# All probabilities of an attention stage turned by VectorE and memory instead of half of them by TensorE

## The reference, cut to what matters

```
x   [16, 256, 256]    ctx [16, 256, 192]    16 heads of 64
q = layernorm(x) @ w_q ; k = ctx @ w_k ; v = ctx @ w_v
attn = softmax(q k^T / 8)                     # per sample and head [256, 256]
x = x + (attn @ v) @ w_o + b_o
x = x + ffn(layernorm(x))                     # 8 experts, the top 2 of each token, 640 slots an expert
```

## Time and profile before

| what | value |
|---|---|
| median of three runs | 955.93 us |
| the profiled execution | 957.82 us, its span 956.1 us, granted clock 0.992 |
| TensorE busy | 918.1 us (96%) |
| VectorE busy | 739.8 us (77%) |
| ScalarE busy | 573.8 us (60%) |
| GpSimd busy | 280.2 us (29%) |
| DMA queue of the SP (and any other hardware queue) | 122.87 MB, 42.9% of 16 engines' span |

### The profile page before, as it was taken

One profiled execution on the slowest core, in us unless ns is written; L12 is line 12 of the kernel. 1 busy time (PEld: TensorE's weight loads), 2 busy tenths in 40 slices (PEclk: granted clock), 3 DMA queues, 4 the chain that ended last, 5 costly groups with the idle time before them and its releaser, 6 DMA issues.

```text
span 956.1 us, 22462 instructions
## 1 busy us (share of the span) xinstructions
PE 918.1 (96%) x7916; PEld 821.0 (86%) x7916; DVE 739.8 (77%) x1745; ACT 573.8 (60%) x1600; POOL 280.2 (29%) x441
## 2 busy tenths in 40 slices
PE   7999999999999999999999999999889999999995
PEld 7878888888888888888888888888689999999995
DVE  5757778888888888888888888877777877678762
ACT  5877766667667666766766677676534433334420
POOL 5541112314233231323223132302533223322233
PEclk9999999999999999999999999999899999999999
DMA  8462535445455445455444445444345765645422
GB/s 239 143 205 91 163 123 163 162 152 168 146 157 158 148 157 164 136 172 164 139 156 161 146 130 170 136 134 136 121 133 99 149 145 123 135 84 98 112 29 27
DMA packets 152991, 133.29 MB, mean 139 GB/s; under 512 B 62140, under 2 KB 141610, under 8 KB 152752
## 3 DMA queue, kind: packets, MB, share of 16 engines
q1 hardware_dynamic: 144048, 122.87, 42.9%
q0 software_dynamic: 8832, 8.98, 5.4%
HBM read 82.15 MB, written 54.61 MB: 143 GB/s over the span
## 4 chain that ended last, share of the span: by engine, by line
PE 70%; DVE 11%; ACT 10%; issue 4%; DMA 3%; POOL 0%; SPq 0%; POOLq 0%; ACTq 0%; DVEq 0%
PE psum L734 20%; PE psum L839 9%; PE psum L996 9%; PE psum L855 9%; PE psum L980 8%; PE psum L801 7%; ACT prob L1067 6%; PE psum L819 5%; DVE negmax L1255 3%; DVE hidl L1201 2%; DVE bufl L1201 1%; ACT probt L1007 1%; DVE hidh L1488 1%; PE psum L879 1%; DVE psum L1274 1%
## 5 line engine op out<-in xcount | busy, mean ns | idle before, releaser
L1067 ACT ACTIVATE prob<-psum,negmax 128x256 f32<-128x256 f32 x512 | 238.0, 481 | 79.5 <-DVE negmax L1255 79.4
L1255 DVE TENSOR_REDUCE negmax<-psum 128x2 f32<-128x512 f32 x256 | 160.4, 682 | 29.7 <-PE psum L801 29.7
L1173 ACT ACTIVATE hid<-psum,b1t 128x640 f32<-128x640 f32 x64 | 50.9, 795 | 126.6 <-PE psum L980 125.0
L839 PE MATMUL psum<-probt,v 128*64 128x256 f32 x1024 | 124.6, 385 | 0.0
L707 POOL DMA_INDIRECT out_rows<-y,rowi x40 | 66.3, 1658 | 160.8 <-DVE y L1498 154.2
L1067 ACT ACTIVATION_READ_ACCUMULATOR prob<-psum,negmax 128x1 f32 x512 | 109.5, 214 | 0.0
L839 PEld LDWEIGHTS psum<-probt,v 128*64 128x64 f32 x1024 | 67.8, 136 | 36.4 <-issue 0.3
L668 POOL DMA_INDIRECT slot_table<-row,picki x64 | 66.8, 1044 | 96.9 <-PE psum L734 61.2
L996 PE MATMUL psum<-w2h,hidh 128*128 128x256 f32 x320 | 91.4, 286 | 2.9 <-DVE y L1498 1.5
L801 PE MATMUL psum<-kh,qh 64*128 64x256 f32 x512 | 82.5, 316 | 11.1 <-ACT prob L1067 8.9
L996 PE MATMUL psum<-w2l,hidh 128*128 128x256 f32 x320 | 90.5, 283 | 0.0
(11 more groups left out here) (199 smaller groups left out, 2704.6 us busy)
## 6 DMA issues: line engine op xcount, KB each, us to landing
squares<-prob SPq DMA_DIRECT2D x56, 512.0 KB
probt<-squares SPq DMA_DIRECT2D x224, 128.0 KB, 2.8
invrows<-inverses SPq DMA_DIRECT2D x128, 128.0 KB
w1r<-in_w SPq DMA_DIRECT2D x8, 1024.0 KB
w2r<-in_w SPq DMA_DIRECT2D x8, 1024.0 KB, 9.1
slot_table<-blank SPq DMA_DIRECT2D x8, 662.5 KB, 6.5
blocks<-slot_table SPq DMA_DIRECT2D x56, 80.0 KB
xin<-in_x SPq DMA_DIRECT2D x16, 256.0 KB, 3.5
```

The lines of the kernel that those rows point to most:

```text
L839: mm = pe.matmul(dst[h * HD:(h + 1) * HD, cc * S:(cc + 1) * S], v[:, b % 2, kb, cols], p, start=(kb == 0), stop=(kb == ST - 1))
L1067: last = act.activation(into, out_of, ACT.Exp, bias=negmax[:, m % 2, u, qb:qb + 1], accum_out=total[:, m % 2, u, qb:qb + 1])
L1255: dve.tensor_reduce(negmax[:, m % 2, u, :], psum[:, u, :].rearrange("p (q s) -> p q s", q=ST), AX.X, ALU.max, negate=True).then_inc(sem("m ...
```

## The change

Every unit of a period in `MOVED` is now turned by VectorE and memory; `by_pe` returns no unit there. What goes with it:

- `turn2`, `turn3`, `copy2`, `copy3` are gone from these periods. `square(m, pair)` transposes two units at once (1024 columns instead of 512), `lift` writes all four (1 MB instead of 512 KB), and each DMA of the move has 256 KB instead of 128 KB.
- The move of period m is issued in period m+1, two of its DMAs by SP (`move_low`, after `inv_out`) and two by ScalarE (`move_high`, between `q_hi` and `exp2`). The lift is now SP's last step of a period, behind `inv_in`; the residual traffic stands between the move and `inv_in`.
- `exps` waits for the lift of m-2, not for its move.
- `a_norm` writes to a new SBUF tensor `attended` (one buffer) instead of back to PSUM, stands behind `k_lo`, and waits for the `a_lo` of the period before. `a_hi` is copied from `attended`, behind `exp3`. `a_lo` of periods 4 to 59 is done by GpSimd.
- `ln1` from the third batch on and all of `pick` but its two reductions (`extremes`) go to GpSimd as well.
- Bank 4, where the turns were, becomes a fourth work bank; `places()` gives the banks out in turn and `pv`'s bank is free after `a_norm` instead of `a_lo`. `logits` uses a work bank too. `pv(m-2)` stands behind `k(m+1)` on TensorE.
- `c0`, `c1` have one buffer instead of two; the scatter waits for `k` instead of `q`.

The diff, cut to its core:

```diff
 def by_pe(m):
-    return (2, 3) if m in MOVED else (0, 1, 2, 3)
+    return () if m in MOVED else (0, 1, 2, 3)
...
         else:
-            out += [("q", m + 1), ("turn2", m - 1), ("k", m + 1), ("turn3", m - 1), ("v", m)]
+            out += [("scores", m)] + ([("logits", b - 2)] if r == 3 and 2 <= b else [])
+            out += [("q", m + 1), ("k", m + 1), ("pv", m - 2), ("v", m)]
...
         else:
-            out += [("copy2", m - 1), ("k_hi", m + 1), ("exp2", m), ("copy3", m - 1), ("exp3", m), ("v_sb", m)]
+            out += [*steps("exp0 exp1", m), ("q_hi", m + 1), ("move_high", m - 1), ("exp2", m), ("k_hi", m + 1), ("exp3", m),
+                    ("a_hi", m - 2), ("v_sb", m)]
...
+        else:
+            out += [("inv", m - 1)] + ([("slot", b - 3)] if r == 2 and 3 <= b else [])
+            out += [("bias", b - 2)] if r == 3 and 2 <= b else []
+            out += [("q_lo", m + 1), ("square0", m), ("k_lo", m + 1), ("a_norm", m - 2)]
         out += [("square1", m)] if m in MOVED else []
...
+        out += [("ln1", b + 1)] if r == 0 and 1 <= b < B - 1 else []
         out += [("scatter", b - 4)] if r == 0 and 4 <= b else []
         out += [("residual", b + 1)] if r == 0 and 1 <= b < B - 1 else []
+        out += [("a_lo", m - 2)] if m - 2 in POOL_REST else []
...
-        out += steps("inv_out inv_in", m - 1) + (steps("lift move", m) if m in MOVED else [])
+        out += [("inv_out", m - 1)] + ([("move_low", m - 1)] if m - 1 in MOVED else [])
+        out += [("traffic", b - 2)] if r == 1 and 2 <= b else []
+        out += [("inv_in", m - 1)] + ([("lift", m)] if m in MOVED else [])
...
+        def move(eng, m, groups):
+            eng.wait_ge(sem("lifted"), 16 * (m - MOVED[0] + 1))
+            eng.wait_ge(sem("pv"), m - 1)
+            for g in groups:
+                eng.dma_start(probt_all(m)[g * SQ:(g + 1) * SQ, :].rearrange("j (a c) -> j a c", a=GROUPS),
+                              square_table[m % 2].rearrange("(a j) (g c) -> g j a c", a=GROUPS, g=GROUPS)[g])\
+                   .then_inc(sem(f"moved{m % 2}"), 16)
...
-                sp.dma_start(square_table[m % 2], prob_pair(m)).then_inc(sem("lifted"), 16)
+                sp.dma_start(square_table[m % 2], prob_all(m)).then_inc(sem("lifted"), 16)
...
+            def a_lo(m):
+                pool.wait_ge(sem("a_hi"), m + 1)
...
+                pool.tensor_tensor(al[:, b % 2, c:c + 2, :], attended[:, :, :],
+                                   ah[:, b % 2, c:c + 2, :].bitcast(F32), ALU.subtract).then_inc(sem("a_lo"), 1)
...
-                if m >= 2 and u in by_pe(m - 2):
+                if m >= 2 and m - 2 not in MOVED:
                     act.wait_ge(sem("turn"), turns_to(m - 2, u))
                 elif m >= 2:
-                    act.wait_ge(sem(f"moved{m % 2}"), 16 * moves_to(m - 2))
+                    act.wait_ge(sem("lifted"), 16 * (m - 2 - MOVED[0] + 1))
...
                 dve.wait_ge(sem("inv_in"), 32 * (m + 1))
-                dve.tensor_tensor(at, at, invrows[:, :, :], ALU.mult).then_inc(sem("a_norm"), 1)
+                if m >= 1:
+                    dve.wait_ge(sem("a_lo"), m)
+                dve.tensor_tensor(attended[:, :, :], work_bank("pv", m).rearrange("p (c s) -> p c s", c=2),
+                                  invrows[:, :, :], ALU.mult).then_inc(sem("a_norm"), 1)
...
-                at = prob_pair(m).rearrange("p (g u c) -> p u g c", g=GROUPS, u=2)[:, u]
+                dve.wait_ge(sem("exp"), UNITS * m + 2 * pair + 2)
+                at = prob_all(m).rearrange("p (g v c) -> p v g c", g=GROUPS, v=2)[:, pair]
                 dve.transpose(at, at).then_inc(sem("square"), 1)
```

More of the change, by code:

```diff
@@ L118, in timeline @@
         out += [("pos", b - 3)] if r == 1 and 3 <= b else []
-        out += steps("exp0 exp1", m) + ([("a_hi", m - 2)] if m >= 2 else []) + [("q_hi", m + 1)]
         if four:
+            out += steps("exp0 exp1", m) + ([("a_hi", m - 2)] if m >= 2 else []) + [("q_hi", m + 1)]
             out += [("copy0", m - 1), ("exp2", m), ("k_hi", m + 1), ("copy1", m - 1), ("exp3", m), ("copy2", m - 1),
@@ L182, in timeline @@
             ("logits_part", o1), ("spread", 0), ("spread", 1), ("pos", e), ("base", 0), ("spread", 2), ("spread", 3)]
[L183 to L184 removed]
+    out += [*steps("exp0 exp1", m), ("q_hi", z), ("move_high", m - 1), ("exp2", m), ("k_hi", z), ("exp3", m), ("a_hi", m - 2), ("v_sb", m), ("x2t_sb", c), ("w_hi", 0), ("w_hi", 1),
             *steps("exp0 exp1", z), ("a_hi", m - 1), ("copy0", m), ("exp2", z), ("copy1", m),
@@ L228, with places @@
 WORKS = [w for w in WORKS if w not in APART]
-WORK_READ = {"xt": "xt_lo", "q": "q_lo", "k": "k_lo", "v": "v_sb", "pv": "a_lo", "o": "x2", "x2t": "x2t_sb",
+WORK_READ = {"xt": "xt_lo", "q": "q_lo", "k": "k_lo", "v": "v_sb", "pv": "a_norm", "o": "x2", "x2t": "x2t_sb",
              "logits": "biased", "pos": "slots"}
+def places():
+    banks, last, found = [5, 6, 7], {}, {}
+    for stage, n in TIMELINE:
+        work = stage.removesuffix("_most"), n
+        if (stage, n) == ("turn0", PERIODS - 2):
+            banks.remove(4)
+            found[stage, n] = 4, last[4]
+        if work in WORKS and work not in found:
+            at = banks.pop(0)
+            banks.append(at)
+            found[work] = at, last.get(at)
+            last[at] = work
+        if (stage, n) == ("turn3", MOVED[0] - 1):
+            banks.append(4)
+    return found
+PLACES = places()
 def build(nc, x, ctxt, wq, wk, wv, wo, bo, rw, rb, w1, b1, w2, b2, out):
@@ L685, in _ @@
                     inverse_root(stage[:3], n)
+                if stage == "ln1" and n >= 2:
+                    ln1(n)
+                if stage == "a_lo" and n in POOL_REST:
+                    a_lo(n)
+                if stage == "pick" and n < B - 4:
+                    pick_(n)
                 if stage == "vsplit":
@@ L1453, in _ @@
             for stage, n in TIMELINE:
-                if stage in steps:
+                if stage in steps and not (stage == "ln1" and n >= 2 or stage == "a_lo" and n in POOL_REST
+                                               or stage == "pick" and n < B - 4):
                     steps[stage](n)
```

174 lines of the change are left out of this document (97 added, 77 removed).

## The result

The changed kernel takes **1038.78 us** (median of four runs, 1029.57 to 1042.66); the kernel before took 955.52 beside it. The ratio is **1.0859** (95% interval 1.0784 to 1.0934): 8.6% slower, where 951 with a range to 986 was forecast.

What follows compares the result with a forecast made beforehand. The prediction took TensorE to bound the kernel before, then a loop through the lift: periods of 10.3, 10.8, 10.5 and 10.1 make 41.7 us a batch against 42.03, saving 4.6 us over 14 batches: 951 us, range 920 to 986.

Steps and rivals of the forecast that it cites:

- the circle: Loop from one move's issue through ScalarE, VectorE, SP and the lift to the next move: 10.1 us a period.
- TensorE's pace: Rival: TensorE still bounds after losing its turns, 38.5 us a batch, 907 us in all; chance 0.05.
- VectorE's sum: VectorE's work per batch: larger squares offset by work given to GpSimd, staying near 35.5 us of 42.
- the way from move to lift: Move's release to lift's issue, through ScalarE's issues, exp2, k_hi, then k_lo, a_norm, inv_in: 5.1 us with semaphores.
- the way from lift to move: Issue of the 1 MB lift to issue of the next move: 5.0 us, from 3.65 for 512 KB.
- The price by bytes: Lift's second 512 KB priced at the 386 GB/s seen in the middle of a lift: 1.36 us more.
- I take 0.7, nearer 0, as the engines are half idle: Delay of one lift a batch by 768 KB of residual traffic ahead of inv_in, bounded by 0 and 2.0 us.
- The share of 0.51: Share of the 16 DMA engines already in use before the change, about half the time over a batch.
- VectorE's own loop: Second loop in VectorE's order: 7.8 us plus small steps; 10.3 us where m mod 4 = 0, 10.5 where 2.
- the lift lands later: Rival: doubled bytes on shared DMA engines make lifts exceed 5.2 us; at 5.7, 982 us; chance 0.30.
- The GpSimd rival: VectorE's a_norm waits for GpSimd's late a_lo, stuck behind scatters and residual; 1 us late gives 965 us; chance 0.07.
- By bytes that becomes about 0.8: Within the late-lift rival: the DMA engines' busy share rises from 0.51 to about 0.8 with twice the bytes.

Runs made afterwards that it cites:

- e10: Kernel of e9 with ScalarE's half of the move left out, so half of the turned probabilities are never read back: 899.99 us, ratio 0.9428.
- e2: Changed kernel with the residual traffic issued behind the lift instead of ahead of inv_in, in periods with m mod 4 = 1: 1018.89 us, ratio 1.0674.
- e3: Changed kernel with VectorE applying ln2 ahead of k_lo instead of behind square1, in periods with m mod 4 = 2: 1007.66 us, ratio 1.0559.
- e11: Changed kernel with 12 identity transposes on TensorE that compute nothing, ahead of x2t's wait for ln2: 1019.20 us, ratio 1.0668.
- e4: Changed kernel with a_lo on VectorE again, behind square1; ln1 and pick stay on GpSimd: 1044.29 us, ratio 1.0925.
- e9: Kernel of e7, plus GpSimd's a_lo ahead of the scatters (periods with m mod 4 = 0) and a_hi ahead of move_high: 980.12 us, ratio 1.0274.
- e12: Changed kernel with only GpSimd's a_lo put ahead of the scatters, in periods with m mod 4 = 0: 1047.47 us, ratio 1.0958.
- e7: Changed kernel with the edits of e2 and e3, and move_high behind exp3 instead of ahead of exp2: 975.08 us, ratio 1.0210.
- e1: Changed kernel with all four pieces of the move issued by SP, none by ScalarE: 1016.04 us, ratio 1.0651.

## Why the prediction was wrong

**Right: TensorE does not set the pace any more, and the circle does, in three of its four steps.** The chain, the waits and the landings show it. The price of TensorE's pace was right as well: 38.06 us a batch in e10, where 38.5 was worked out, and 900 us against 907.

**Right: VectorE's sum** is 35.96 us a batch (35.57 before), the square 1.24, a_lo 1.28.

**Nearly right: the way from move to lift**, 5.5 us in the mean where 5.1 was summed; 1.7 us a batch.

**Wrong, the step that failed: the way from lift to move, "Then the lift itself", with 5.0.** It is 6.5 in the mean. Three parts:
- r3 and r0 took 5.2 and 5.8. The price by bytes was short by 0.2 to 0.8; why r0's lift lands 0.5 us later than r3's stays open. The Trainium skill's fit ("DMA: Bandwidth & Descriptors", Anatomy of one DMA) with 4.4 was further off than the rows' 5.0; the page gives it for DMAs that GpSimd issues, and SP issues these.
- r1: "I take 0.7, nearer 0, as the engines are half idle". It was 1.8 (e2), near the bound of 2.0. The share of 0.51 was a batch's mean, and from the kernel before. In the stretch in question, the 4.8 us ahead of r1's lift, the engines are full (1.02 from 398.5 to 403.3). A mean share says when nothing is missing over a batch; it does not say that there is room at a given place.
- r2: 8.0, of which 3 us were no lift at all (it landed after 4.8; e3). The prediction closed VectorE's own loop with ln2 in r2 as a small step behind square1 and priced its length, 10.5 us for the step where 13.3 was measured. It did not ask who waits for ln2: TensorE's x2t, and behind it the scores of r3. With the circle late, that small step came late, and the clock fell on top (20 us by e11).

These terms close the sum: the measured 48.2 us a batch is 6.5 over the forecast's 41.7, 91 us in 14 batches, and 951 + 91 = 1042.

**The rival "the lift lands later"**, chance 0.30, with 982 us at 5.7 us a lift, had the direction and a part of the size. Lifts landed after 5.25 us in the mean of r0, r2 and r3, and the traffic added 1.8 in r1. By the rival's own rule that is 4 x (5.1 + 5.25) + 1.8 = 43.2 us a batch, and some 972 us. The other 5 us a batch are no later lift: 1.7 between move and lift, and 3.2 in r2 by which ScalarE came behind the landing.

**The GpSimd rival** saw waits that exist. Taking them out made no kernel faster (e4, e9, e12), and none of these runs isolates their price.

**Not foreseen: what comes behind the circle.** "By bytes that becomes about 0.8" was right (0.75 here, 0.83 in e7), and was not followed up: lift after move, each waiting for the other. In the circle shown the engines are full for 8 us and nearly empty for 2 us at its turn (0.03 from 384 to 386), and from move to move it takes 11.3 us, where 10.1 was forecast.

## What to carry to other kernels

Price a transfer in the stretch in which it runs, with what was issued just ahead of it on the same engines, never by a mean share; and when a round trip is hung on an engine that runs its program in order, list who waits for each step queued behind the wait, also on the engine that was the bound. A round trip that takes over all of the work can lose where three quarters of it gain: look for the share at which the engine relieved and the resource loaded end together.

## What the runs showed of the hardware

Two queues made the issues parallel, not the transfers. A piece of the move landed after 4.9 us (median) from one queue (e1), and after 4.8 and 5.1 from two. The Trainium skill ("DMA: Bandwidth & Descriptors", Issuing engines are not separate DMA queues) says that DMAs of all issuing engines run on the same 16 engines, and that a second issuer saves issuing time only; the runs agree.

GpSimd's a_lo held VectorE's ln2 up. The instructions of ln2 in the changed kernel, in ns (min, median, max):

```profile
L1287 DVE TENSOR_SCALAR row<-x,ln_mean_var,ln_rstd x30: 401/407/1150, 124.3 to 772.2; 128x256 f32<-128x256 f32 x30
```

The first ln2 of a batch starts 0.27 us after GpSimd's a_lo and takes 1.14 to 1.15 us, 13 times of 13, and ends 0.15 us after a_lo's end; the next one takes 0.40. With a_lo on VectorE (e4) all of them take 0.40 to 0.41. The Trainium skill ("SBUF — State Buffer", Who interferes with whom) calls it an exclusive lock: a tensor_scalar of VectorE can run in a two-port mode, and then it or a GpSimd instruction, whichever starts first, keeps the shared ports to its end. The rows agree in that ln2 ended just behind a_lo each time. The prediction used the rule for a_lo's duration only; it bit on VectorE's side, 0.74 us a batch, on the way to x2t.

GpSimd's ln1 takes 1.23 us (median) for 256 columns, where VectorE's took 0.41 before.
